# Filling TensorE's pauses with products whose results nobody reads

## The chip, the cores and the metric

The kernel runs on one core of a Trainium2 chip. The metric is the device time of one execution in microseconds. Three timed runs stand for the kernel before: 1015.5, 1013.42 and 1009.02 us, median 1013.42 us.

## The reference, cut to what matters

The kernel computes eight residual layers over x and a context, both 32 x 64 rows of 128 features (2048 tokens): `x = x + layer(layernorm(x), ...)`. In order they are: attention with 16 small heads (A0), a feed-forward layer (F0), attention with 16 heads of 64 (A1), a mixture of 16 experts (E1), two mixtures of eight experts of which every token takes two (E2, E3), attention with 16 small heads under a mask (A3), and a quantised feed-forward layer (Q3). The change sits ahead of E2, in and ahead of E3, and ahead of A3. The two expert layers are, in short:

```
# E2: the routing looks at the context, not at x
logits = context @ Wg + bg                      # 2048 x 8
top 2 of the logits, softmax over the two -> combine
y = relu(x @ W1[e] + b1[e]) @ W2[e] + b2[e];  out = sum_e combine[e] * y[e]
# E3: the routing looks at x
logits = x @ w_router.T;  top 2, weights normalised -> combine
y = (silu(x @ w_gate[e].T) * (x @ w_up[e].T)) @ w_down[e].T
out = sum_e combine[e] * y[e]
# A3: q = x @ Wq.T, k, v = context @ Wk.T, Wv.T; masked softmax attention; @ Wo.T
```

All inputs are float32.

## The kernel before

The 2048 tokens are 16 tiles of 128 tokens (NT), in four groups of four tiles (NG groups of GW = 512 columns). X keeps the residual stream with tokens on the partitions; `ctxT` keeps the context turned, features on the partitions; `ident` is the 128 x 128 identity. Every engine has its own instruction list, written out in full in the order given by hand; engines wait for each other by semaphores only (`wait_ge`), and a waiting instruction holds up everything behind it on its engine. There are eight PSUM banks; `m.banks[4]` is the fifth.

**Layers E2 and E3** are both built by `dispatched_experts`. Each token's two copies are sorted by expert into 39 tiles of 128 rows (NTILE). The normalised rows are stored to DRAM by SyncE's queue, and GpSimd fetches the rows of one tile with an indirect DMA (`fetch`, L2214), three tiles ahead. Per tile TensorE turns the rows (`turn`, L2094), multiplies them by the first weights of the tile's expert (`first`, L2098: four 128-column products in E2, six in E3), and, one tile later, the hidden rows by the last weights (`second`, L2123). VectorE and ScalarE copy the turned rows and the expert's weights, apply the activation and copy the result, and GpSimd sends it to DRAM with an indirect DMA (`send`, L2222). A float32 product shows as two MATMUL records in the trace. At the end SyncE reads the results back, and VectorE adds them to X group by group (L2305), with the next layer's norm statistics between the groups.

For E2 the tables of the routing (which token sits in which row) were made long before, beside F0. For E3 they depend on x, and are made between the layers, in this order on TensorE (the block `if gated:` of `tensor`, from L2075): `m.ahead.keys` (four 512-column products for the keys of A3, banks 2 to 5, copied out by ScalarE at L555), then per group g a turn of the normalised rows (L220, waits for VectorE's `xn`) and four logit products of 8 columns each (L1797, wait for ScalarE's copy of the turned rows, L228); `rank_products` (L1849 to L1851, wait for VectorE's choice of the best two, until L1828); `m.ahead.values` (L569); and `table_products` four times (L1914, eight 40-column products each). Table j waits for GpSimd's `owners` (L1906), which waits for VectorE's `places` (L1894, L1898); `places` of j = 2 and 3 wait for `ab_used` of table j - 2, because two buffers take turns. After the last table ScalarE copies it out (`owner`, L1920), VectorE makes the indices, GpSimd issues the first fetch (671.15 us in the profile), and TensorE waits for those rows in `turn(0)`.

**A3**, `prepared_attention`: TensorE first waits until E3 has written its last output, then takes per group a turn of the normalised rows (L220) and one 512-column product (L632), `queries(g)`, with the scores of tiles 0 and 1 (L642, L648) between them; after that the tiles follow in a steady order.

Of the kernel before, what the change touches and what calls it, by code (L numbers as in the profile page):

```python
# [18 lines left out]
NG = NT // GT  # L19
GW = GT * P  # L20
# [12 lines left out]
def live(t):  # L33

    return not isinstance(t, int) or 0 <= t < NT


def past(t, k):

    return not isinstance(t, int) or t >= k  # L40
# [7 lines left out]
def pipeline(eng, step, lo, hi, end, first=0):  # L48

    for n in range(first, lo):  # L50
        step(n, n % 2)
    with eng.Fori(lo, hi - 1, 2) as i:
        step(i, lo % 2)
        step(i + 1, (lo + 1) % 2)
    for n in range(hi, end):
        step(n, n % 2)
# [18 lines left out]
def apart(eng, m):  # L75


    eng.sem_inc(m.passed, 1)


class Signal:
# [43 lines left out]
class Norm:  # L125
# [10 lines left out]
    def stats(self, dve, x, t, p):  # L136
        if past(t, 2):
            dve.wait_ge(*self.rstd_ready(t - 1))
        dve.bn_stats(self.st[:, p, :], x).then_inc(self.stats_chain.sem, 1)
        dve.wait_ge(*self.stats_chain(2 * t + 1))  # L140
        apart(dve, self)
        dve.bn_aggr(self.mv[:, p, :], self.st[:, p, :]).then_inc(self.stats_chain.sem, 1)
        dve.wait_ge(*self.stats_chain(2 * t + 2))
        dve.tensor_scalar(self.ve[:, p, :], self.mv[:, p, 1:2], EPS, None, ALU.add).then_inc(self.var_ready.sem, 1)  # L144
# [435 lines left out]
def prepared_attention(sh, m, tag, masks, w, ahead):  # L580
# [42 lines left out]
    def tensor(pe):  # L623
        pe.wait_ge(*free)
        pe.wait_ge(*masks)

        def queries(g):
            norm.turn(pe, g)
            pe.wait_ge(*norm.xnT_ready(g + 1))
            if g >= 2:  # L630
                pe.wait_ge(*q_all(g - 1))
            pe.matmul(m.banks[6 + g % 2], w["q"], m.XNT[:, g * GW:(g + 1) * GW], start=True, stop=True  # L632
                      ).then_inc(q_ps.sem, 1)

        def scores(t, p):
            pe.wait_ge(*qT_ready(t + 1))
            pe.wait_ge(*kexp_ready(t + 1))
            if past(t, 2):
                pe.wait_ge(*sub_ready(t - 1))
            apart(pe, m)  # L640
            for u in range(2):
                pe.matmul(pS[p][:, u, :].rearrange("p (h k) -> p h k", k=S), m.hidden_square[:, :],  # L642
                          m.hidden_keys[:, bass.ds(t, 1), :].broadcast_to([P, HP, S]), start=True, stop=False,
                          skip_group_check=True)
            for b in range(2):
                for u in range(2):
                    rows = slice(u * S, (u + 1) * S)
                    mm = pe.matmul(pS[p][b * S:(b + 1) * S, u, :], qT[rows, p, b * S:(b + 1) * S],  # L648
                                   kexp[rows, p, b].rearrange("p h k -> p (h k)"), start=False, stop=True,
                                   skip_group_check=True)  # L650
            mm.then_inc(scores_ready.sem, 1)

        def turn_out(t, p):
            pe.wait_ge(*on_ready(t + 1))
            if past(t, 1):
                pe.wait_ge(*oT_ready(t))
            pe.transpose(J2[:, 0:P], on[:, p, :], m.ident[:, :]).then_inc(oT_ps.sem, 1)

        def weigh_values(t, p):
            pe.wait_ge(*probT_ready(2 * t + 2))  # L660
            pe.wait_ge(*vbd_ready(2 * t + 2))
            if past(t, 1):
                pe.wait_ge(*on_ready(t))
            for c in range(HP):
                for b in range(2):
                    mm = pe.matmul(pO[b * S:(b + 1) * S, c * 18:c * 18 + 18], probT[:, p, c, b * S:(b + 1) * S],
                                   vbd[:, p, b, 2 * c:2 * c + 2, :].rearrange("p h d -> p (h d)"),
                                   start=True, stop=True)
            mm.then_inc(o_ps.sem, 1)

        def project(t, p):
            pe.wait_ge(*oT_ready(t + 1))
            if past(t, 1):
                pe.wait_ge(*x_done(t))
            pe.matmul(J2[:, P:2 * P], oT[:, p, :], w["o"], start=True, stop=True).then_inc(out_ps.sem, 1)

        def turn_probs(t, p):
            pe.wait_ge(*prob_ready(t + 1))
            if past(t, 1):
                pe.wait_ge(*probT_ready(2 * t))  # L680
            for c in range(HP):
                tr = pe.transpose(pP[:, c // 4, c % 4 * P:c % 4 * P + P],
                                  prob[:, p, 2 * c:2 * c + 2, :].rearrange("p h k -> p (h k)"), m.ident[:, :])
                if c % 4 == 3:
                    tr.then_inc(probT_ps.sem, 1)

        def step(n, p):
            q = 1 - p
            if live(n):
                scores(n, p)  # L690
            if live(n - 3):
                turn_out(n - 3, q)
            if live(n - 2):
                weigh_values(n - 2, p)
            if live(n - 3):
                project(n - 3, q)
            if live(n - 1):
                turn_probs(n - 1, q)

        queries(0)  # L700
        queries(1)
        scores(0, 0)
        queries(2)
        scores(1, 1)
        queries(3)
        pe.wait_ge(*q_all(NG))
        turn_probs(0, 0)
        pipeline(pe, step, LO, HI, END, 2)
# [1291 lines left out]
def dispatched_experts(sh, m, tag, start, spec):  # L2000
# [12 lines left out]
    E, C, gated, disp = spec["E"], spec["C"], spec.get("gated"), spec["dispatch"]  # L2013
# [37 lines left out]
    def turned_at(n):  # L2051

        return n - 2 if turns and 0 <= n - 2 < 3 * turns.E else None
# [18 lines left out]
    def tensor(pe):  # L2072
        if spec.get("late"):
            spec["late"].tensor(pe)
        if gated:  # L2075
            m.ahead.keys(pe)
            for g in range(NG):
                norm.turn(pe, g)
                pe.wait_ge(*norm.xnT_ready(g + 1))
                disp.logit_products(pe, J1, m.XNT, spec["wr"], g)  # L2080
            disp.rank_products(pe, J1)
            m.ahead.values(pe)
            for j in range(NCH):
                disp.table_products(pe, J1, j)
            pe.wait_ge(*disp.owner_ready(1))
        m.begin(pe, start)
        pe.wait_ge(*disp.expert_ready(1))
        pe.wait_ge(*spec["weights_here"])

        def turn(i):  # L2090
            pe.wait_ge(*x_here[i % 4](16 * (i // 4 + 1)))
            if i >= 2:
                pe.wait_ge(*xT_ready(i - 1))
            pe.transpose(T[i % 2][:, 0:P], xg[:, i % 4, :], m.ident[:, :]).then_inc(xT_ps.sem, 1)  # L2094

        def products(out, p, k0):
            for c in range(C):
                mm = pe.matmul(out[:, c * P:(c + 1) * P], WE[:, p, (k0 + c) * P:(k0 + c + 1) * P], XT[:, p, :],  # L2098
                               start=True, stop=True)
            mm.then_inc(a_ps.sem, 1)  # L2100

        def first(i):
            p = i % 2
            pe.wait_ge(*xT_ready(i + 1))
            pe.wait_ge(*w_ready(i + 1))
            if gated:
                if i >= 2:
                    pe.wait_ge(*h_ready(i - 1))
                products(m.banks[2 + p], p, 0)
                products(m.banks[4 + p], p, C)  # L2110
            else:
                if i >= 3:
                    pe.wait_ge(*h_ready(i - 2))
                products(m.banks[2 + i % 3], p, 0)

        def second(i):
            p = i % 2
            e = pe.value_load(disp.expert[0:1, i:i + 1], min_val=0, max_val=E - 1)
            pe.wait_ge(*h_ready(i + 1))
            if i >= 2:  # L2120
                pe.wait_ge(*y_out(i - 1))
            for c in range(C):
                mm = pe.matmul(Y[p][:, 0:P], h[:, p, c, :],  # L2123
                               W2[:, bass.ds(e, 1), c, :].rearrange("p o d -> p (o d)"),
                               start=c == 0, stop=c == C - 1)
            mm.then_inc(y_ps.sem, 1)

        turn(0)
        for i in range(NTILE):
            first(i)  # L2130
            if i + 1 < NTILE:
                turn(i + 1)
            if i >= 1:
                second(i - 1)
            if turned_at(i) is not None:
                turns.turn(pe, turned_at(i))
        second(NTILE - 1)
# [895 lines left out]
```

## Time and profile before

| | us |
|---|---|
| median of the three runs (lowest, highest) | 1013.42 (1009.02, 1015.5) |
| the profiled execution | 1012.4 |
| its span, first to last instruction | 1010.6 |
| mean granted TensorE clock | 0.883 of full speed |
| TensorE busy (matmuls) / weight loads | 785.4 / 647.6 |
| VectorE / ScalarE / GpSimd busy | 617.2 / 468.1 / 373.9 |

The span is cut by TensorE's clock into stretches at 1.00 (2.4 GHz) and at 0.50 (1.2 GHz); a mean between the two in a row says that the clock changed in it. In the timeline view each row is one instruction or a run of equal ones: start, duration, engine, source line, what it writes and reads, count, and in brackets the idle time of the engine before it with what ended it. Times are counted from the first instruction of the span. What a product "costs" TensorE is read from the spacing of successive records, since records overlap.

### The profile page before, as it was taken

What the parts mean: (1) busy time and instruction counts of PE and PEld (TensorE: products, weight loads), DVE (VectorE), ACT (ScalarE), POOL (GpSimd) and SP (SyncE); (2) the same over time, 40 slices, a digit from 0 to 9 for tenths busy, and PEclk for the clock granted to TensorE, in tenths of its full rate; (3) what the DMA queues carried; (4) which work ended last, traced back from release to release, by engine and by line L of the source; (5) the groups of instructions that cost most, each with busy time, mean ns of one, the idle gap of its engine ahead of it and who ended that gap; (6) DMA issues with size and microseconds to landing.
All of it is one profiled execution on the core that took longest, in us unless ns stands there. A gap on an engine that the chain in (4) does not pass through costs nothing.

```text
span 1010.6 us, 24103 instructions
## 1 busy us (share of the span) xinstructions
PE 785.4 (78%) x8041; PEld 647.6 (64%) x8041; DVE 617.2 (61%) x1610; ACT 468.1 (46%) x928; POOL 373.9 (37%) x492
## 2 busy tenths in 40 slices
PE   6998898999999789996477765567878469969005
PEld 3776787888888679985476663567777426643005
DVE  3886747777777667767353324642222378867795
ACT  3886434555444344442154433034554237735753
POOL 5663421111111331111566662146666445550800
PEclk9999699999999979999699998569999779978557
DMA  6300000000000000023333213101111300000001
GB/s 186 97 0 1 1 1 3 2 3 1 0 0 3 1 9 21 20 102 103 95 104 87 61 44 102 42 17 40 43 43 44 96 11 3 0 1 1 0 0 42
DMA packets 49218, 36.06 MB, mean 36 GB/s; under 512 B 7665, under 2 KB 44978, under 8 KB 49138
## 3 DMA queue, kind: packets, MB, share of 16 engines
q1 hardware_dynamic: 43420, 24.45, 8.6%
q0 software_dynamic: 4992, 10.23, 3.7%
q8 instruction: 48, 0.79, 0.3%
q10 hardware_dynamic: 726, 0.33, 0.1%
q14 instruction: 32, 0.26, 0.1%
HBM read 26.73 MB, written 8.26 MB: 35 GB/s over the span
## 4 chain that ended last, share of the span: by engine, by line
PE 66%; DVE 12%; issue 6%; another core or an unknown queue 5%; ACT 4%; DMA 3%; DVEq 2%; POOL 2%; ACTq 1%; SPq 0%; POOLq 0%
PE psum L2098 9%; PE psum L1448 7%; PE psum L2123 3%; PE psum L1018 3%; PE psum L960 3%; PE psum L938 3%; PE psum L923 3%; PE psum L2398 2%; PE psum L1415 2%; PE psum L1416 2%; PE psum L1417 2%; PE psum L308 2%; PE psum L1000 2%; PE psum L648 2%
## 5 line engine op out<-in xcount | busy, mean ns | idle before, releaser
L2098 PE MATMUL psum<-E_XT,E_weights 128*128 128x128 f32 x780 | 115.4, 300 | 48.7 <-DVE E_XT L2250 20.0
L2098 PEld LDWEIGHTS psum<-E_XT,E_weights 128*128 128x128 f32 x780 | 103.5, 209 | 58.3 <-DVE E_XT L2250 24.3
L2222 POOL DMA_INDIRECT y_scratch<-E_y,route_place_of x78 | 78.8, 1010 | 78.2 <-DVE E_y L2275 33.1
L2214 POOL DMA_INDIRECT E_rows<-rows_scratch,route_token_of x78 | 76.4, 979 | 31.8 <-issue 25.9
L1707 DVE SCALAR_TENSOR_TENSOR X<-psum,E_gates,X 128x128 f32<-128x128 f32 x256 | 71.7, 344 | 26.3 <-PE psum L1448 26.2
L1448 PEld LDWEIGHTS psum<-E_w,E_h 128*128 128x128 f32 x512 | 69.4, 198 | 11.6 <-issue 3.5
L2178 ACT ACTIVATE E_h<-psum,cols 128x128 f32<-128x128 f32 x156 | 44.6, 368 | 67.0 <-PE psum L2098 45.8
L1532 ACT ACTIVATE E_h<-psum,cols 128x512 f32<-128x512 f32 x64 | 43.9, 689 | 67.4 <-PE psum L1417 67.4
L1448 PE MATMUL psum<-E_w,E_h 128*128 128x128 f32 x512 | 70.3, 282 | 4.8 <-DVE X L1707 3.8
L2265 DVE TENSOR_TENSOR E_h<-E_sg,psum 128x384 f32<-128x384 f32 x39 | 21.6, 554 | 72.7 <-PE psum L2098 27.7
L203 POOL TENSOR_TENSOR rstd<-vareps,nhalf 128x4 f32<-128x4 f32 x24 | 24.7, 1032 | 81.7 <-DVE vareps L197 81.5
L220 PE MATMUL psum<-ident,xn 128*128 128x128 f32 x80 | 19.6, 392 | 39.7 <-DVE xn L211 29.5
L150 POOL TENSOR_TENSOR A_A_inner_rstd<-A_A_inner_vareps,nhalf 128x1 f32<-128x1 f32 x16 | 8.7, 544 | 95.5 <-DVE A_A_inner_vareps L144 95.5
L2123 PE MATMUL psum<-L1w,E_h 128*128 x312 | 43.5, 284 | 0.5 <-DVE E_y L2277 0.5
L220 PEld LDWEIGHTS psum<-ident,xn 128*128 128x128 f32 x80 | 13.3, 202 | 47.0 <-issue 23.2
L2387 PE MATMUL psum<-ident,Q_amax_rows 128*1 128x128 f32 x5 | 1.8, 352 | 52.3 <-DVE Q_amax_rows L2495 51.6
L773 POOL TENSOR_TENSOR A_kexp<-E_first,hmask 128x512 f32<-128x512 f32 x32 | 32.6, 1042 | 25.8 <-PE psum L648 25.7
L2123 PEld LDWEIGHTS psum<-L1w,E_h 128*128 128x128 f32 x312 | 39.5, 198 | 1.1 <-issue 0.7
L2094 PE MATMUL psum<-ident,E_rows 128*128 128x128 f32 x78 | 22.9, 294 | 22.2 <-DMA E_rows<-rows_scratch,route_token_of 22.2
L2161 ACT ACTIVATE E_weights<-E_first 128x768 f32 x39 | 32.9, 843 | 14.0 <-issue 13.7
L2277 DVE TENSOR_TENSOR E_y<-psum,E2b2all 128x128 f32<-128x128 f32 x39 | 11.3, 290 | 44.7 <-PE psum L2123 19.8
L1563 POOL CAST E_WH<-E_w 128x128 fp32r<-128x128 f32 x16 | 4.6, 290 | 90.9 <-DMA E_w<-in_L_ffn_routed_w 72.3
(342 smaller groups left out, 2156.1 us busy)
## 6 DMA issues: line engine op xcount, KB each, us to landing
routed_back<-y_scratch SPq DMA_DIRECT2D x16, 256.0 KB, 4.9
E_first<-in_L_xattn_W SPq DMA_DIRECT2D x1, 2048.0 KB, 8.5
L1w<-in_L_xattn_W SPq DMA_DIRECT2D x8, 256.0 KB, 4.5
rows_scratch<-xn SPq DMA_DIRECT2D x8, 256.0 KB, 2.3
E_w<-in_L_ffn_routed_w SPq DMA_DIRECT2D x28, 64.0 KB, 1.8
E_raw<-in_L_ffn_w_down SPq DMA_DIRECT2D x8, 176.0 KB
E_rows<-rows_scratch,route_token_of POOLq DMA_INDIRECT x78
y_scratch<-E_y,route_place_of POOLq DMA_INDIRECT x78
```

The lines of the kernel that those rows point to most:

```text
L220: tr = pe.transpose(self.bank[:, i * P:(i + 1) * P], self.m.xn[:, g * GT + i, :], self.m.ident[:, :])
L773: ke = pool.tensor_tensor(kexp[:, p, b], kk.broadcast_to([P, HP, S]), m.hmask[:, :].rearrange("p (h o) -> p h o", o=1).broadcast_to([P, HP ...
L923: mm = pe.matmul((J1, J0)[j][:, c * P:(c + 1) * P], w["k"][:, cc * P:(cc + 1) * P], columns(m.ctxT, t, P), start=True, stop=True)
L1448: mm = pe.matmul(y_bank(e, g)[:, i * P:(i + 1) * P], h[:, g % 2, c, i * P:(i + 1) * P], w2[:, p, c, :], start=(c == 0 and i == 0), stop=(c ...
L1532: act.activation(h[:, g % 2, c, :], ring[(C * g + c) % 4], spec["func"], bias=spec["b1"][:, bass.ds(e * C + c, 1)]).then_inc(h_ready.sem, 1)
L1707: st = dve.scalar_tensor_tensor(out=m.X[:, t, :], in0=y_bank(e, g)[:, i * P:(i + 1) * P], scalar=gates[:, t, bass.ds(e, 1)], in1=m.X[:, t, :],
L2098: mm = pe.matmul(out[:, c * P:(c + 1) * P], WE[:, p, (k0 + c) * P:(k0 + c + 1) * P], XT[:, p, :], start=True, stop=True)
L2123: mm = pe.matmul(Y[p][:, 0:P], h[:, p, c, :], W2[:, bass.ds(e, 1), c, :].rearrange("p o d -> p (o d)"), start=c == 0, stop=c == C - 1)
L2161: act.activation(WE[:, i % 2, :], W1[:, bass.ds(e, 1), :].rearrange("p o f -> p (o f)"), ACT.Copy).then_inc(w_ready.sem, 1)
L2178: ac = act.activation(h[:, p, c, :], m.banks[2 + i % 3][:, c * P:(c + 1) * P], spec["func"], bias=spec["b1"][:, bass.ds(e * C + c, 1)])
L2214: pool.indirect_dma_start(out=xg[:, i % 4, :], out_offset=None, in_=rows[:, :], in_offset=bass.IndirectOffsetOnAxis(ap=disp.token_of[:, i: ...
L2222: pool.indirect_dma_start(out=yrows[:, :], in_=y[:, i % 3, :], in_offset=None, out_offset=bass.IndirectOffsetOnAxis(ap=disp.place_of[:, i: ...
```

## The change

A helper issues n products `ident x ctxT[:, 0:512]` into bank 4, float32, each a start and a stop, with no semaphore. Nobody reads the result. It is called at nine places of TensorE's list. One wait is added, for ScalarE's copy of the four key blocks, ahead of the first products of E3's block, since bank 4 holds one of those blocks.

```diff
--- before.py
+++ after.py
@@ -76,6 +76,12 @@
 
 
     eng.sem_inc(m.passed, 1)
+
+
+def idle_products(pe, m, n):
+
+    for _ in range(n):
+        pe.matmul(m.banks[4], m.ident[:, :], m.ctxT[:, 0:GW], start=True, stop=True)
 
 
 class Signal:
@@ -697,7 +703,9 @@
             if live(n - 1):
                 turn_probs(n - 1, q)
 
+        idle_products(pe, m, 12)
         queries(0)
+        idle_products(pe, m, 2)
         queries(1)
         scores(0, 0)
         queries(2)
@@ -2074,13 +2082,19 @@
             spec["late"].tensor(pe)
         if gated:
             m.ahead.keys(pe)
+            pe.wait_ge(*m.ahead.k_ready(NG))
+            idle_products(pe, m, 8)
             for g in range(NG):
+                idle_products(pe, m, (0, 2, 2, 0)[g])
                 norm.turn(pe, g)
                 pe.wait_ge(*norm.xnT_ready(g + 1))
                 disp.logit_products(pe, J1, m.XNT, spec["wr"], g)
+            idle_products(pe, m, 5)
             disp.rank_products(pe, J1)
             m.ahead.values(pe)
             for j in range(NCH):
+                if j:
+                    idle_products(pe, m, 2)
                 disp.table_products(pe, J1, j)
             pe.wait_ge(*disp.owner_ready(1))
         m.begin(pe, start)
@@ -2125,6 +2139,7 @@
                                start=c == 0, stop=c == C - 1)
             mm.then_inc(y_ps.sem, 1)
 
+        idle_products(pe, m, 6 if gated else 12)
         turn(0)
         for i in range(NTILE):
             first(i)
```

In the last hunk E3 (gated) gets 6 products and E2 gets 12.

## Rows read from the trace of the kernel before

**Rows 1.** The page: granted TensorE clock in 40 slices, and chain shares by engine.

```profile
PEclk9999699999999979999699998569999779978557
...
PE 66%; DVE 12%; issue 6%; another core or an unknown queue 5%; ACT 4%; DMA 3%; DVEq 2%; POOL 2%; ACTq 1%; SPq 0%; POOLq 0%
```

**Rows 2.** Busy time by stretch (us, instructions), PEclk the mean clock; half-clock stretches.

```profile
475.50:499.40 23.90, 6.62 (x28) 5.96 (x29) 11.68 (x43) 2.29 (x8) 9.99 (x9) 0.50 0.38 106
...
799.80:823.70 23.90, 7.94 (x18) 3.40 (x22) 18.18 (x83) 2.39 (x4) 10.39 (x15) 0.50 0.33 91
sum 95.60, PE 40.94 PEld 33.04 DVE 57.76 ACT 13.74 POOL 31.23; mean PE 10.23 PEld 8.26 DVE 14.44 ACT 3.44 POOL 7.81
```

**Rows 3.** The same view, of pauses of TensorE that began at full clock.

```profile
366.90:370.00 3.10, 0.09 (x1) 0.12 (x1) 2.85 (x12) 1.92 (x3) 0.74 (x2) 0.95 0.15 42
...
742.10:745.30 3.20, 0.48 (x3) 0.49 (x4) 0.56 (x1) 0.94 (x3) 2.00 (x3) 0.98 0.13 41
...
583.40:586.10 2.70, 0.26 (x2) 0.27 (x3) 0.97 (x3) 0.53 (x3) 1.87 (x2) 1.00 0.16 49
```

**Rows 4.** Timeline (start us, us, engine, line, instruction, [idle before]), start of layer E2.

```profile
478.73 1.11 DVE L1707 SCALAR_TENSOR_TENSOR X<-psum,E_gates,X 128x128 f32<-128x128 f32 x4
...
492.02 0.45 PE L2094 MATMUL psum<-ident,E_rows 128*128 128x128 f32 x1 [18.04 <-DMA E_rows<-rows_scratch,route_token_of]
...
492.84 2.08 PE L2098 MATMUL psum<-E_XT,E_weights 128*128 128x128 f32 x8 [0.38 <-DVE E_XT L2250]
...
497.60 1.92 PE L2123 MATMUL psum<-L1w,E_h 128*128 x8
...
500.24 1.01 POOL L2222 DMA_INDIRECT y_scratch<-E_y,route_place_of  x1 [3.89 <-DVE E_y L2277]
```

**Rows 5.** Timeline: four 512-column products at full clock.

```profile
618.93 3.70 PE L549 MATMUL psum<-ctxT,L3w 128*128 128x512 f32 x8 [0.58 <-ACT qw_down L2661]
```

**Rows 6.** Busy time by stretch, of 512-column products that began at half clock.

```profile
910.40:915.80 5.40, 5.31 (x7) 2.21 (x8) 2.80 (x8) 1.19 (x2) 0.00 (x0) 0.50 0.00 0
```

**Rows 7.** Timeline of the routing ahead of layer E3 and of its first tile.

```profile
622.67 0.60 ACT L555 ACTIVATE E_first<-psum 128x512 f32<-128x512 f32 x1 [0.26 <-PE psum L549]
...
632.12 1.12 PE L220 MATMUL psum<-ident,xn 128*128 128x128 f32 x4 [9.48 <-DVE xn L211]
...
641.64 1.11 PE L220 MATMUL psum<-ident,xn 128*128 128x128 f32 x4 [1.09 <-DVE xn L211]
...
646.95 1.87 PE L1797 MATMUL psum<-cols,XNT 128*128 128x8 f32 x8 [0.69 <-ACT XNT L228]
...
653.97 0.80 PE L1849 MATMUL psum<-route_both,earlier 128*128 128x128 f32 x2 [5.15 <-DVE route_ahead L1828]
...
655.35 5.96 PE L569 MATMUL psum<-L3w,ctxT 128*64 128x64 f32 x128
...
661.75 1.07 PE L1914 MATMUL psum<-route_A,route_B 128*128 128x40 f32 x8 [0.44 <-POOL route_A L1906]
...
666.28 3.39 PE L1914 MATMUL psum<-route_A,route_B 128*128 128x40 f32 x16 [2.13 <-POOL route_A L1906]
...
673.87 0.45 PE L2094 MATMUL psum<-ident,E_rows 128*128 128x128 f32 x1 [4.21 <-DMA E_rows<-rows_scratch,route_token_of]
...
674.69 2.93 PE L2098 MATMUL psum<-E_XT,E_weights 128*128 128x128 f32 x12 [0.37 <-ACT E_XT L2155]
...
681.41 1.50 PE L2098 MATMUL psum<-E_XT,E_weights 128*128 128x128 f32 x12
```

**Rows 8.** Timeline, start of the last attention.

```profile
813.56 1.09 PE L220 MATMUL psum<-ident,xn 128*128 128x128 f32 x4 [15.95 <-DVE xn L211]
...
820.03 2.07 PE L632 MATMUL psum<-XNT,L3w 128*128 128x512 f32 x2 [0.69 <-ACT XNT L228]
...
824.26 0.66 PE L220 MATMUL psum<-ident,xn 128*128 128x128 f32 x4
...
825.61 1.12 PE L632 MATMUL psum<-XNT,L3w 128*128 128x512 f32 x2 [0.69 <-ACT XNT L228]
```

## The prediction

> **What bounds the kernel now.** I began with the page. In the chain that ended last, TensorE holds 66% of the span, and its granted clock is at full speed in most slices but low in some [rows 1]. So a lower clock can cost time only where TensorE's own work lies on that chain, and the next view asks how much of it there is. The view by stretch, over the four half-clock stretches next to the changed places (475.5 to 499.4, 625.7 to 659.8, 666.6 to 680.3, 799.8 to 823.7 us), shows 95.6 us, of which TensorE works 40.9 us [rows 2]. In the rest it waits: for row fetches, for VectorE's norms, for VectorE's and GpSimd's routing chain. If all 40.9 us were at full clock and all of it on the chain, 20.4 us would be saved. That is the ceiling, and the added products have to be paid out of it.
>
> Next, what comes before a fall. TensorE's last product before E2 ended at 474.0 (492.02 less 18.04 of idle, [rows 4]) and the clock was at half from 475.5 [rows 2]. Pauses of 3.1 us (366.8) and 2.8 us (742.0) end with the mean clock just under 1.00: it had fallen by their end. A pause of 2.5 us (583.3) passed at 1.00 [rows 3]. I read it so: a pause of 3 us or more mostly costs the clock, one of 2 to 2.5 us sometimes. And a rise: 512-column products begun at half clock ran 5.4 us without one [rows 6], and E2's first tiles from 492.0 ran until 499.4, 7.4 us [rows 2, 4]. I take 5 us of dense products before a rise, between 2.5 (no row excludes half of rows 6) and 7.4.
>
> **Price of one product.** Four of the same shape took 3.70 us at full clock [rows 5]: 0.86 us each without the tail of the last. At half clock seven records started in 5.4 us, two records a product [rows 6]: 1.72 us each. Twelve take 10.3 us at full, 20.6 at half. If they start at half and the clock rises after t us, they take 10.3 + t/2. Nobody reads them, but TensorE works in order: whatever does not fit the pause delays the real work behind it, and half clock doubles the overhang.
>
> **E2, 12 products.** TensorE is let go when the last update of X ends, 479.9 [rows 4], at half clock, and its rows arrive at 492.02: 12.1 us. With t = 5 the products end at 492.7, 0.7 us late (t = 2.5: 0.4 early, so on time; t = 7.4: 1.9 late; no rise: 8.5 late). At full clock the first tiles gain: twelve records take 1.50 instead of 2.93 us [rows 7], so eight gain 0.95, and two firsts (2.08 each) and one second (1.92) lie in a row to the first output [rows 4]: 2.8 us. GpSimd's first send waited 3.89 us for that output, and its later fetches stand behind that send [rows 4], so the gain is kept. Net -2.0, ends -2.8 and +7.
>
> **Keys, 8 products and the added wait.** The keys are copied out at 623.3 [rows 7]. Still at full clock, eight products end at 630.2; the first turn waits for VectorE until 632.12 [rows 7]. Cost nothing, covered by that pause. The wait holds only the products; the pause hides it.
>
> **Logits, 0/2/2/0.** On the path are the last two groups, from the turn at 641.64 to the last logit at 648.8 [rows 7]. At full clock the turn takes 0.66 instead of 1.11 [rows 7, 8]; the 8-column logits, 1.87 at half, come near the table products, eight narrow records in 1.07 [rows 7]: I take 1.0. Twice both: -2.6. But from 630.2 to 634.4 TensorE has only a turn and narrow products, so the clock may fall; then the two products ahead of group 2 take 3.4 us where the pause was 1.09 [rows 7], 2.3 late. Between -2.6 and +2.3 I take -1.0, nearer to full clock because products of group 1 follow.
>
> **Rank, 5 products.** The pause is 5.15 us [rows 7]; 4.3 fit at full, 8.6 at half are 3.4 late, and full clock saves 0.6 of the small products. Between -0.6 and +3.4: +0.3.
>
> **Tables, 2 products ahead of each but the first.** This is the step that decides. The values (128 records, 5.96 us mostly at half) become about 3 us at full, but the first table still waits for VectorE and GpSimd, 7.8 us behind the rank products (653.97 to 661.75, [rows 7]). A new pause of about 3 us opens, of the kind after which the clock had fallen [rows 3]. Then the pairs stand in the way: before, table 1 followed table 0 at once, and all four took from 661.75 to 669.67, 7.9 us, the last two at half [rows 7]. Tables now, at full throughout: 4 x 1.07 + 3 x 1.72 = 9.4, +1.5. At half throughout: 4 x 1.70 + 3 x 3.44 = 17.1, +9.2 (16 records in 3.39, [rows 7]). With a rise after 5 us, behind the first pair: 1.7 + 3.44 + 3 x 1.07 + 2 x 1.72 = 11.8, +3.9. I take +3.9; the ends are +1.5 and +9.2. Behind them wait ScalarE's copy, VectorE's indices and GpSimd's first fetch. Even at full clock this step loses.
>
> **E3, 6 products.** The pause is 4.21 us [rows 7]; 5.2 at full is 1.0 late, 10.3 at half 6.1 late: +1.1. The first tile's product falls from 2.93 to 1.50 [rows 7], partly hidden behind ScalarE's activation: -1.0 (ends 0 and -2.8, with the second tile).
>
> **A3, 12 and 2 products.** TensorE is free at 797.6 (813.56 less 15.95, [rows 8]). At full clock twelve end by 808.3. The turn waits until 813.56, a pause of 5.2 us, longer than those after which the clock had fallen: it starts at half as before. Turn, query product and the pair fill from there, so the rise comes near 819 instead of 823.7 [rows 2]; the pair (begun near 817.0) makes the second turn, at 818.2 before, some 1.5 us late. From there to the third turn, 824.26, half-clock work on the path shrinks by about 2.2 us (0.45 for a turn, 0.95 for a product, 2.07 against 1.12, the rest scores) [rows 8]. Net -0.7, ends -2.0 (clock held) and +2.2 (no rise sooner).
>
> **Sum.** -2.0 - 1.0 + 0.3 + 3.9 + 1.1 - 1.0 - 0.7 = +0.6 us, on the profiled execution's 1012.4 (span 1010.6 and 1.8 around it): 1013.0. That execution lies 1.0 below the median of the three runs, which is what is predicted: 1014.0.
>
> **A rule against the rows.** Rows first: of the 95.6 us at half, TensorE works 40.9 [rows 2]. The Trainium skill, page "TensorE: Matmul & The Clock Gate", section "Terms", says the penalty is about the throttled time times (1 - K/N). By that rule, an estimate, these four stretches cost 47.8 us and the time without them would be near 966 us.
>
> **Rivals.**
> *The clock is held.* If narrow products and short pauses do not let it fall, every stage ends at its low end: -2.8 (E2), -2.6 and -0.6 (routing), +1.5 (tables), +1.0 - 1.4 (E3), -2.0 (A3): -6.9, 1006.5. For it: pauses of 2.5 us passed [rows 3]. Against it: the pauses of 3 us before the tables and 5.2 us in A3 stay. 20%.
> *Slower: the half clock meets the products of the routing.* Place: from the logits of group 2 to the last table. If the clock falls between 630.2 and 641.6 and is back only in the tables: +2.3, +3.4, +3.9, +1.1 - 1.0, with -2.0 and -0.7 elsewhere: +7.0, 1020.4. It decides as soon as the pair ahead of group 2 runs at half. If the tables stay at half as well, 5.3 more and six products at half, 5.1 more: 1031. For it: the trace has half clock in all of this stretch. Against it: the products themselves are dense. 18%, of which 5% for the longer form.
> *All half-clock work was on the chain.* Then 20.4 us go: 993.6. Against it stand the waits of rows 4 and 7. The same rule of the skill points this way, only further. 3%.
> *It doesn't do what it says.* If these products do not raise the clock, E2 is 8.5 late, and the tables and the six products cost 9.2 and 6.1: about +25, 1039. Against it: the same shape stands before the rise of rows 6. 2%.
>
> **How the numbers follow.** My forecast has 57% with its own range of 1010 to 1018.5 (steps' ends, and runs that spread from 1009.0 to 1015.5). The range of 8 in 10 reaches to both rivals: 1007.0 to 1020.0. One per cent, about what a measurement of this kernel can tell from no change, is 10 us: all low ends together give 6.9, so faster 4% (the third rival and a rest); slower 8% (the long form of the second, the fourth and a rest); within 88%.
>
> **What would show it.** In the changed trace: first turn of E2 within 1 us of 492.7 and eight-record products near 1.1 us at once; eight products done 2 us before the first turn of E3's routing; the clock row between rank and tables, at half when the first table starts; more than 9.4 us from the first table's start to the last one's end; the six products overhanging the row fetch; half clock at A3's first turn and a rise before 821. Wrong would be: full clock from 623 to 680 without a break, or a first tile of E2 still at 2.08 us.

## The result and the profile after

The changed kernel took 1021.25 us in the median of 19 runs, the kernel before 1015.61 us in 19 runs on the same chip: ratio 1.0043, 95% interval 1.0029 to 1.0058, or 4.4 us slower (2.9 to 5.9). A second copy of it (below) gave 1.0025 (1.0004 to 1.0046). Ratios and intervals are those of the record, taken over all runs; the quotient of the two medians is 1.0056. The forecast was 0.6 us slower, 1014.0 in a range of 1007.0 to 1020.0; 1013.42 us times the ratio is 1017.8. One run each of two variants below (e2_sixteen, fitted), 1205 us long at a mean clock of 0.63 and 0.64, is left out of their ratios as slow.

First the page of the changed kernel: the granted clock in 40 slices, the chain that ended last by engine, and by line.

```profile
PEclk9999699999999879998999989798899889978557
...
PE 72%; DVE 10%; ACT 4%; issue 4%; another core or an unknown queue 3%; POOL 2%; DMA 2%; DVEq 2%; ACTq 1%; SPq 0%; POOLq 0%
PE psum L2112 10%; PE psum L1456 7%; PE psum L2137 5%; PE psum L84 4%; PE psum L1026 3%; PE psum L968 3%; PE psum L946 3%; PE psum L931 3%; PE psum L2413 2%; PE psum L1423 2%; PE psum L1424 2%; PE psum L1425 2%; PE psum L314 2%; PE psum L1008 2%
...
L84 PE MATMUL psum<-ctxT,ident 128*128 128x512 f32 x110 | 60.0, 700 | 7.3 <-DVE X L1715 5.9
```

The clock is higher than before, 0.906 against 0.883 on average, and TensorE's share of the chain went from 66% [rows 1] to 72%. L84 is the line of the added products: 55 of them, two records each, 60.0 us of TensorE, and 4% of the chain, some 40 us, is the products themselves. Products that nobody reads became part of what sets the time.

Where the half clock was next to the changed places (95.6 us, TensorE at work in 40.9 [rows 2]), the same view of the changed kernel shows this (busy time and records of PE, PEld, DVE, ACT, POOL, then the mean clock):

```profile
478.00:488.20 10.20, 5.97 (x7) 2.52 (x8) 9.43 (x38) 0.00 (x0) 4.03 (x3) 0.50 0.26 77
641.80:645.20 3.40, 3.40 (x7) 1.39 (x6) 3.15 (x16) 0.00 (x0) 1.03 (x1) 0.50 0.11 30
648.60:655.50 6.90, 6.90 (x15) 3.80 (x16) 4.68 (x16) 0.00 (x0) 0.00 (x0) 0.51 0.01 2
665.70:669.10 3.40, 3.40 (x10) 1.86 (x8) 1.24 (x2) 0.00 (x0) 0.72 (x1) 0.50 0.00 0
822.70:829.50 6.80, 6.11 (x12) 2.57 (x11) 6.59 (x29) 1.19 (x2) 2.53 (x3) 0.50 0.00 0
sum 30.70, PE 25.78 PEld 12.14 DVE 25.08 ACT 1.19 POOL 8.31; mean PE 5.16 PEld 2.43 DVE 5.02 ACT 0.24 POOL 1.66
```

65 us of half clock went here, and the kernel became slower. (Over the whole span it is some 45 us less, 237 against 192; the bodies of E2 and E3 have more of it than before, 10.2 and 27.3 us against 3.5 and 17.1.) In the half clock that is left TensorE works 84% of the time, against 43% before. But 20.7 of its 25.8 us are the added products, by the same view of L84 alone:

```profile
sum 30.70, PE 20.67 PEld 7.44; mean PE 4.13 PEld 1.49
```

So the kernel's own work at half clock fell from 40.9 to 5.1 us, and what now runs at half clock is mostly the products themselves, some of them in the way of the chain. The rule of the Trainium skill weighed in the prediction (page "TensorE: Matmul & The Clock Gate", section "Terms") would have it that 64.9 us less throttled time are worth about 32 us, an estimate by that page; no run shows a gain of this size or any gain of the whole change.

The start of E2, TensorE's timeline:

```profile
482.23 13.52 PE L84 MATMUL psum<-ctxT,ident 128*128 128x512 f32 x24 [5.93 <-DVE X L1715]
495.59 0.27 PE L2108 MATMUL psum<-ident,E_rows 128*128 128x128 f32 x1
496.25 1.16 PE L2112 MATMUL psum<-E_XT,E_weights 128*128 128x128 f32 x8 [0.38 <-issue]
...
499.01 1.15 PE L2137 MATMUL psum<-L1w,E_h 128*128 x8
500.05 1.16 PE L2112 MATMUL psum<-E_XT,E_weights 128*128 128x128 f32 x8
```

Against [rows 4], the eight-record products take 1.16 instead of 2.08 us at once. But the turn now has no idle time before it: the twelve products end 13.4 us after E1 does (482.2), where the rows had arrived after 12.2. Then the routing:

```profile
625.96 7.13 PE L84 MATMUL psum<-ctxT,ident 128*128 128x512 f32 x16 [0.69 <-ACT E_first L561]
634.42 0.66 PE L226 MATMUL psum<-ident,xn 128*128 128x128 f32 x4 [1.33 <-DVE xn L217]
...
636.68 1.96 PE L84 MATMUL psum<-ctxT,ident 128*128 128x512 f32 x4
639.19 0.66 PE L226 MATMUL psum<-ident,xn 128*128 128x128 f32 x4 [0.55 <-DVE xn L217]
...
641.45 3.41 PE L84 MATMUL psum<-ctxT,ident 128*128 128x512 f32 x4
644.66 0.88 PE L226 MATMUL psum<-ident,xn 128*128 128x128 f32 x4
...
650.05 7.22 PE L84 MATMUL psum<-ctxT,ident 128*128 128x512 f32 x10
657.11 0.38 PE L1857 MATMUL psum<-route_both,earlier 128*128 128x128 f32 x2
...
657.77 3.95 PE L575 MATMUL psum<-L3w,ctxT 128*64 128x64 f32 x128
664.18 1.07 PE L1922 MATMUL psum<-route_A,route_B 128*128 128x40 f32 x8 [2.46 <-POOL route_A L1914]
665.10 3.17 PE L84 MATMUL psum<-ctxT,ident 128*128 128x512 f32 x4
667.28 2.26 PE L1922 MATMUL psum<-route_A,route_B 128*128 128x40 f32 x8
669.38 1.96 PE L84 MATMUL psum<-ctxT,ident 128*128 128x512 f32 x4
...
673.39 1.37 PE L1922 MATMUL psum<-route_A,route_B 128*128 128x40 f32 x8
675.05 5.42 PE L84 MATMUL psum<-ctxT,ident 128*128 128x512 f32 x12 [0.29 <-ACT route_owner L1928]
680.31 0.27 PE L2108 MATMUL psum<-ident,E_rows 128*128 128x128 f32 x1
680.95 1.60 PE L2112 MATMUL psum<-E_XT,E_weights 128*128 128x128 f32 x12 [0.37 <-ACT E_XT L2170]
```

Only two of these groups of products, the eight and the pair of group 1, leave a pause behind them. The five (7.22 us from start to end, at half clock in large part) run past 655.3, when VectorE had the ranks' operand ready; the values fell from 5.96 [rows 7] to 3.95 us, and the 2.46 us pause that this opens is followed by a fall of the clock at 665.7, in the first pair; the tables last from 664.18 to 674.8, 10.6 us against 7.9 [rows 7].

### The profile page after: what moved, and what is told of

The parts are those of the page before. It is cut to its first block, busy times and chain, and to the rows that moved or that the text cites. A ratio compares the mean times of both kernels' runs of the same rounds, so it can differ in the third digit from the quotient of the medians.

```text
span 1019.7 us, 24322 instructions
## 1 busy us (share of the span) xinstructions
PE 834.9 (82%) x8151; PEld 666.3 (65%) x8151; DVE 617.4 (61%) x1610; ACT 466.8 (46%) x928; POOL 372.5 (37%) x492
## 4 chain that ended last, share of the span: by engine, by line
PE 72%; DVE 10%; ACT 4%; issue 4%; another core or an unknown queue 3%; POOL 2%; DMA 2%; DVEq 2%; ACTq 1%; SPq 0%; POOLq 0%
PE psum L2112 10%; PE psum L1456 7%; PE psum L2137 5%; PE psum L84 4%; PE psum L1026 3%; PE psum L968 3%; PE psum L946 3%; PE psum L931 3%; PE psum L2413 2%; PE psum L1423 2%; PE psum L1424 2%; PE psum L1425 2%; PE psum L314 2%; PE psum L1008 2%
## 5 line engine op out<-in xcount | busy, mean ns | idle before, releaser
L84 PE MATMUL psum<-ctxT,ident 128*128 128x512 f32 x110 | 60.0, 700 | 7.3 <-DVE X L1715 5.9
L84 PEld LDWEIGHTS psum<-ctxT,ident 128*128 128x128 f32 x110 | 23.3, 220 | 35.5 <-issue 26.9
L2292 DVE TENSOR_TENSOR E_y<-psum,E2b2all 128x128 f32<-128x128 f32 x39 | 11.3, 290 | 53.8 <-PE psum L2137 43.2
L156 POOL TENSOR_TENSOR A_A_inner_rstd<-A_A_inner_vareps,nhalf 128x1 f32<-128x1 f32 x16 | 8.7, 543 | 95.6 <-DVE A_A_inner_vareps L150 95.6
L781 POOL TENSOR_TENSOR A_kexp<-E_first,hmask 128x512 f32<-128x512 f32 x32 | 32.6, 1042 | 25.9 <-PE psum L654 25.8
L1067 ACT ACTIVATE A_xnT<-psum,cols 128x128 f32<-128x128 f32 x16 | 7.3, 457 | 65.3 <-PE psum L956 65.3
```

The lines of the kernel that those rows point to most:

```text
L84: pe.matmul(m.banks[4], m.ident[:, :], m.ctxT[:, 0:GW], start=True, stop=True)
L781: ke = pool.tensor_tensor(kexp[:, p, b], kk.broadcast_to([P, HP, S]), m.hmask[:, :].rearrange("p (h o) -> p h o", o=1).broadcast_to([P, HP ...
```

## Experiments

**How they are read.** Every variant was measured beside the kernel before, in five rounds. Besides the ratio, each profile gives the lengths of stages: **start of E2** (end of E1 to the third tile's first product), **body** of E2 and E3 (from there to the last second product), **routing** (end of the keys to E3's third tile), **start of A3** (E3's last second product to the first turned probabilities). The 14 profiles (before, after and twelve variants; two of the twelve are second copies) show how far one profile can be trusted. The part ahead of E2, the same in all, ends between 477.9 and 482.7 us. E2's body is 116.3 to 121.3 us long, E3's 114.4 to 120.3, in kernels with and without products. So the 9.1 us between the spans of the first two profiles (1010.6 and 1019.7) hold 2.3 us from before anything was changed. Part of the scatter of E2's body goes with the clock inside it: the two shortest (116.3 and 117.0 us) have 3.4 and 3.5 us of half clock in them, the two longest (121.2 and 121.3) have 17.1, and over the 14 profiles the correlation is 0.86; for E3's body it is 0.44. Short stretches scatter less and decide below.

**1 to 3. Each place alone.** Theory R put the loss into the routing ahead of E3. Rival B put it into the bodies: what a start gains, the layer's later tiles give back.

```
e2_only:      idle_products(pe, m, 0 if gated else 12)   # nothing else
routing_only: 8 behind keys, (0,2,2,0), 5, 2 if j, 6 ahead of E3
a3_only:      12 ahead of queries(0), 2 ahead of queries(1)
```

> Only the 12 products ahead of layer E2's first turn. Theory R (the loss is made in the routing ahead of E3, the other places gain): from the end of E1 to the start of the third tile's first product 1.5 to 2 us less than in the kernel before (there 19.5 us), E2's body after that as before (117.0 us from that start to the last second product), total -1.5 to -2 us, ratio 0.998. Rival B (an earlier start is given back in the body of a sparse layer, because each of its tiles then meets the clock or a queue at a worse moment): the start gains the same, the body is 1 to 2 us longer, total within 0.5 us of before, ratio 1.000.

> Only the products and the wait between E2 and E3 (8, 2, 2, 5, 2, 2, 2, 6). Theory R: from the end of the keys to the end of the tables 47.0 us becomes 49 to 51, to E3's first turn 51.2 becomes 54 to 56, E3's third tile 2 to 4 us later than before, the body of E3 as before (116.2 us from the third tile's first product to the last second product), total +3 to +4 us, ratio 1.003 to 1.004. Rival B: besides, E3's body is 3 to 4 us longer, total +6 to +8 us, ratio 1.007.

> Only the 12 and 2 products ahead of the last attention's queries. Both theories: the clock falls in the pause that the twelve leave (4.7 us in the changed kernel's trace), the pair delays the second turn by about 2 us, and the earlier rise gives it back: from E3's last product to the first turn of probabilities 33.7 us before, 33.0 to 33.6 now; total -0.7 to 0 us, ratio 0.9995. If the clock is held the same stretch takes 32 us, ratio 0.998.

Measured: e2_only 1.0009 (0.9989 to 1.0029), routing_only 1.0010 (0.9991 to 1.0029), a3_only 1.0007 (0.9986 to 1.0027). No ratio differs from 1, and their sum, +2.6 us, is compatible with the whole. Two forecasts were missed: e2_only did not gain its 1.5 to 2 us (0.998), and the routing alone, forecast at 1.003 to 1.004, has an interval that ends at 1.0029. So these three ratios do not place the loss. The stages say more. e2_only: start 17.8 us against 19.5 before, body 121.2 against 117.0. That looked like rival B, but a3_only, where E2 is untouched, had a body of 120.0. routing_only: routing 60.9 against 58.8.

**4. Without the pairs between the tables.**

```
-                if j:
-                    idle_products(pe, m, 2)
```

> The changed kernel without the pairs of products between the four tables; all else stays. Theory R: the four tables, 10.6 us in the changed kernel's trace (7.9 before), take 6 to 8 us again, E3's first turn comes 3 us earlier than in the changed kernel, total 3 us below it, ratio to before 1.001. Rival B: E3's body stays 3 to 4 us longer than before, total 2 to 4 us above before, ratio 1.003.

Measured: 1.0007 (0.9992 to 1.0023) against 1.0043 with them. The three pairs cost 3.6 us, the difference of these ratios, 2.1 either way by their two intervals; against the second copy (1.0025) it is 1.8, 2.7 either way, so the time alone does not fix the size. The tables' own length does it better: 10.6, 10.6 and 13.9 us in the three profiles with the pairs, 7.9 to 8.1 in the ten without products there. From table 0 to the end of the tables it is 8.0 us again here. Something is given back, though: from the end of the tables to E3's third tile 13.1 us against 11.6 with the pairs.

**5. The kernel before again.** One comment added.

> The kernel before once more, only a comment added. Nothing can differ, so it says what the profiled body of a sparse layer (from the third tile's first product to the last second product) is from one execution to the next. Theory N (the bodies fall into patterns of their own that differ by chance): ratio within 0.2% of 1; E2's body between 116.9 and 121.3 us, and not the 116.98 us of the first profile except by luck. Rival B (an earlier start of E2 is given back in its body, by a wait that the start had covered): E2's body within 0.5 us of 116.98 us, since the start is not moved.

Measured: 0.9997 (0.9977 to 1.0017). E2's body: 119.3 us, 2.3 more than in the first profile of the same code. Rival B's evidence, one body against another, is gone; most of that difference goes with the half clock in the body (3.5 us in the first profile, 13.7 here, 17.1 in e2_only). The start of E2, too, moved without products: 18.4 us instead of 19.5. The clock rose 17.1 us after E1's end and not 19.6: in the second of three half-clock products.

**6. Twelve products ahead of E2, again.**

> Only the twelve products ahead of E2, once more. Theory N: the first product of the third tile again 1.3 us nearer to the end of E1 than before (about 17.8 us), the body anywhere between 117 and 121.3 us, the time on average 1.3 us shorter: ratio 0.9987, and with the first run of it an interval that still holds that. Rival B: the body again 121 us or more, the ratio at or above 1.000.

Measured: 0.9988 (0.9968 to 1.0009); with e2_only a mean of 0.9999, about 0.0014 either way, which neither shows nor excludes a gain of 1.3 us. Start 17.8, body 118.3.

**7. Fours between the tables, nothing else.**

```
+                if j:
+                    idle_products(pe, m, 4)
```

> Only the products between the tables, and four instead of two ahead of the second, third and fourth table; nothing elsewhere. Theory R (the pairs between the tables are the loss): twelve products in the way of the tables instead of six. 12 x 0.86 = 10.3 us at full clock, less the 3.7 us or so that faster tables give back, so 6 to 9 us slower: ratio 1.006 to 1.009, and keys' end to tables' end 53 to 56 us against 47.0 before. Rival (E2's and E3's bodies decide, the pairs hardly count): less than 3 us slower, ratio under 1.003.

Measured: 1.0061 (1.0040 to 1.0082), 6.2 us slower; end of the keys to end of the tables 54.9 us against 47.0. Both numbers are as Theory R had them, but of the 7.9 us 1.7 arose ahead of any added product: VectorE waited 7.88 us for the rows read back, not 6.16, and TensorE's first turn came later, as this kernel's rows show. The first is to be held against the 9.48 us of [rows 7]:

```profile
634.66 1.12 PE L226 MATMUL psum<-ident,xn 128*128 128x128 f32 x4 [11.21 <-DVE xn L217]
664.29 1.07 PE L1920 MATMUL psum<-route_A,route_B 128*128 128x40 f32 x8 [1.50 <-POOL route_A L1912]
676.98 1.36 PE L1920 MATMUL psum<-route_A,route_B 128*128 128x40 f32 x8
```

The tables themselves took 14.1 us, 5.9 more than the 8.1 of most profiles without products there, and this agrees with the 6.2 us of time. Products between the tables go into the time.

**8. Fitted to the pauses of the changed profile.**

```
A3: 12 and 2 -> 17 and 0;  E3: 6 -> 4;  routing: none;  E2: 12
```

> A version fitted to the pauses that the profile after shows: twelve products ahead of E2, none in the routing, four ahead of E3, seventeen ahead of the first query turn of the last attention (the pause from 807.0 to 822.3 us holds 17 x 0.86 = 14.6 us) and none ahead of the second. Theory R: E2 -1.3, E3's four products at the fetch wait 0 to +0.5 with a first tile 1 us faster, A3 -1.5 to -2: 1 to 4 us faster than before, ratio 0.996 to 0.999. Rival B (what a start gains the body gives back): ratio 1.000 +/- 0.001.

Measured: 1.0002 (0.9977 to 1.0026); the gain forecast did not come. In the last attention the seventeen did what they were to do, TensorE's timeline:

```profile
798.07 14.86 PE L84 MATMUL psum<-ctxT,ident 128*128 128x512 f32 x34 [0.38 <-DVE E_y L2283]
813.35 0.66 PE L226 MATMUL psum<-ident,xn 128*128 128x128 f32 x4 [0.43 <-DVE xn L217]
814.70 1.13 PE L638 MATMUL psum<-XNT,L3w 128*128 128x512 f32 x2 [0.69 <-ACT XNT L234]
818.12 1.11 PE L226 MATMUL psum<-ident,xn 128*128 128x128 f32 x4 [2.30 <-DVE xn L217]
...
824.66 0.66 PE L226 MATMUL psum<-ident,xn 128*128 128x128 f32 x4
```

The first query product takes 1.13 us, not 2.07, and all it buys is a longer wait for VectorE: 2.30 us ahead of the second turn. The third turn comes 27.0 us after E3's last product; before, 26.7. VectorE's timeline of the kernel before says why:

```profile
821.86 2.36 DVE L211 TENSOR_SCALAR xn<-X,meanvar,rstd 128x128 f32<-128x128 f32 x8
824.48 1.22 DVE L837 TENSOR_REDUCE A_mx<-psum 128x16 f32<-128x1024 f32 x1 [0.25 <-PE psum L648]
```

VectorE is busy with the norms until 824.2 and takes up the scores 0.25 us later. Up to that point all of TensorE's half-clock work had at most 0.25 us to give.

**9. Sixteen ahead of E2.** The question is whether a shift of the start reaches the end.

```
idle_products(pe, m, 0 if gated else 16)   # nothing else
```

> Only products ahead of E2, sixteen instead of twelve, so that the first turn comes 4 x 0.86 = 3.4 us later than with twelve. With twelve the third tile's first product began 17.8 us after the end of E1 in every profile, in those without products 18.4 to 19.5; with sixteen it should be at 21.2. Rival B (the start of E2 is not what paces its body, so a shift of the start is taken back within some tiles): the fourteenth tile's first product at 53.7 to 55 us after the end of E1, as in all profiles so far with and without products (53.7 to 54.6), and the time within 2 us of before, ratio 0.999 to 1.002. Theory K (a shift of the start is kept): the fourteenth tile at 57 us or more, 3.4 us slower than with twelve, ratio about 1.003.

Measured: 1.0033 (1.0013 to 1.0053), 3.3 us slower; the third tile at 21.2, the fourteenth at 56.9 against 52.8 to 54.6 in all others. Rival B falls: a delay of E2's start is kept. What of a gain? With twelve or ten products the third tile comes at 17.6 to 17.9 us in all seven profiles (mean 17.8), without them at 18.4 to 19.5 (six profiles, mean 19.1): 1.3 us. At the fourteenth tile the means are 53.8 and 54.3, so 0.6 us of the 1.3 is still there.

**10. The six products ahead of E3, alone.**

```
idle_products(pe, m, 6 if gated else 0)    # nothing else
```

> Only the six products ahead of E3. Forecast term: they end 1 us after the rows would have let the first turn start and the first tiles gain 1.0, net +0.1. Theory R: from the end of the tables to the third tile's first product 11 to 12 us, as in the profiles without them (10.7 to 11.7), ratio 1.000 +/- 0.001. Rival (the six products run at half clock, in which case they take 10.3 us against a pause of 4.2): that stretch 13 us or more, as in the profile without the table pairs (13.1), ratio 1.001 to 1.002, and E3's body a matter of chance (114.4 to 120.3 us so far) in both.

Measured: 1.0032 (1.0010 to 1.0054), 3.2 us slower: the rival by its stretch (14.0 us from the end of the tables to the third tile), and above the 1.001 to 1.002 that it gave for the time. Stretches with the six products in this kernel, and then in the changed one (the mean clock stands behind the five busy times):

```profile
669.90:677.70 7.80, 7.73 (x13) 3.28 (x13) 1.08 (x6) 0.86 (x2) 3.91 (x4) 0.68 0.16 36
```

```profile
675.00:680.40 5.40, 5.35 (x13) 2.34 (x13) 1.07 (x6) 0.84 (x1) 3.24 (x4) 1.00 0.09 24
```

The same six products take 5.4 us at full clock and 7.8 from half. From GpSimd's first fetch to the first turn: 2.7 us without them, 4.1 in the changed kernel, 6.5 here; the first tiles give back 1.0 in both. With the pairs between the tables, which cost 3.6, the six ran at full clock; without them part of the six ran at half (5.6 us from the first fetch in experiment 4). This is what was given back there.

**11. What seemed worth having.**

```
E2: 10;  keys: 8;  logits: (0,2,2,0);  rank, tables, E3, A3: none
```

> What the profiles so far leave as worth having: ten products ahead of E2 (with twelve the first turn started as the last of them ended, 1.2 us after the rows would have let it), eight behind the keys and 0/2/2/0 ahead of the groups of logits, and none ahead of rank, tables, E3 and the last attention. Theory R: from the end of the keys to the end of the logits 24.9 to 25.1 us as with those products before (25.7 to 26.2 without), and with nothing ahead of rank the gain reaches the end of the tables: 45.8 us against 46.7 to 47.3. Third tile of E2 at 16.2 to 17 us after E1's end. If all of it is kept, 1.1 + 2.2 us faster, ratio 0.997; if E2's share is given back in the body (Rival B), 1.1 us, ratio 0.999.

Measured: 0.9978 (0.9956 to 1.0000), 2.2 us faster at the edge of what five rounds tell, and the only variant whose whole interval lies at or below 1. Its profile shows two things. With ten products the first turn comes 12.1 us after E1's end and not 13.4, yet the third tile is at 17.6, as with twelve. VectorE's copy of the third tile's rows, in this kernel and then in e2_again:

```profile
497.63 0.29 DVE L2260 COPY E_XT<-psum 128x128 f32<-128x128 f32 x1 [1.95 <-remote]
```

```profile
497.69 0.29 DVE L2257 COPY E_XT<-psum 128x128 f32<-128x128 f32 x1 [0.66 <-PE psum L2100]
```

Both start 17.3 to 17.4 us after E1's end (480.36 and 480.28), against 17.7 to 18.0 in the profiles without products there. ScalarE's next activation starts with them, at 497.71 and 497.76, though its products had ended at 496.0 and 497.1. In all seven profiles with twelve or ten products it is 17.3 to 17.5, wherever the first turn was. Two engines are held there together, and the profile does not name the source. The expectation of 16.2 to 17 us for the third tile was missed by this. And the logits, TensorE's timeline:

```profile
623.02 7.13 PE L84 MATMUL psum<-ctxT,ident 128*128 128x512 f32 x16 [0.69 <-ACT E_first L561]
...
632.90 1.76 PE L1803 MATMUL psum<-cols,XNT 128*128 128x8 f32 x8 [0.69 <-ACT XNT L234]
634.51 3.76 PE L84 MATMUL psum<-ctxT,ident 128*128 128x512 f32 x4
638.06 1.06 PE L226 MATMUL psum<-ident,xn 128*128 128x128 f32 x4
639.81 1.87 PE L1803 MATMUL psum<-cols,XNT 128*128 128x8 f32 x8 [0.69 <-ACT XNT L234]
641.54 3.76 PE L84 MATMUL psum<-ctxT,ident 128*128 128x512 f32 x4
```

Here both pairs ran at half clock (3.76 us, not 1.96), and the logits ended 27.8 us after the keys, where 24.9 to 25.1 was expected and 25.9 is usual without products: the same products that gained 0.8 to 1.8 us in four other profiles lost 1.9 in this one. (This is the profiled execution, 1013.3 us; the median of this variant's runs is 1010.3.)

**12. The changed kernel again.**

> The changed kernel once more, only a comment added. Theory R: ratio 1.003 to 1.006 again; from the end of the keys to E3's third tile 61 us (58.3 on average without the products); E3's start to the last attention's first turned probabilities 33.5 to 34.2 us as in every profile. The bodies of E2 (116.99 to 121.28 so far) and E3 (114.35 to 120.29) anywhere in their spread; Rival (the products lengthen E3's body, 120.29 in the first profile of it): E3's body at 118 or more again.

Measured: 1.0025 (1.0004 to 1.0046). Routing 62.6 us; E3's body 116.3, so the rival on that body is not borne out; start of A3 33.5. The tables of this execution:

```profile
657.58 1.52 PE L1922 MATMUL psum<-route_A,route_B 128*128 128x40 f32 x8 [2.46 <-POOL route_A L1914]
658.93 3.76 PE L84 MATMUL psum<-ctxT,ident 128*128 128x512 f32 x4
661.70 2.52 PE L1922 MATMUL psum<-route_A,route_B 128*128 128x40 f32 x8
664.05 3.76 PE L84 MATMUL psum<-ctxT,ident 128*128 128x512 f32 x4
...
670.14 1.36 PE L1922 MATMUL psum<-route_A,route_B 128*128 128x40 f32 x8
```

Two pairs at half clock, 13.9 us for the tables, where the first profile had one and 10.6.

## Why the prediction was right, and where its sizes were off

The mechanism held: less half clock, no time gained, and the loss in the routing, most of it between the tables. This rests on experiments 4, 7 and 10 and on the lengths of stages; the routing alone (1.0010) does not show it in time. The time was missed by 4 us (2 by the second copy). Taken term by term, with the mean of the profiles that have a set of products and of those that lack it:

| term | forecast | measured |
|---|---|---|
| E2, 12 products | -2.0 | -1.3 at the third tile, -0.6 at the fourteenth; in time, over both runs, -0.2, 1.4 either way |
| keys, 8 products and the wait | 0 | 0: done 1.3 us before the first turn |
| logits | -1.0 | -1.3 in four profiles, +1.9 in one, against those without products (table_fours, with its late rows, left out) |
| rank, 5 products | +0.3 | +1.3 |
| values at full clock, to table 0 | 0 | -0.7 |
| pairs between the tables | +3.9 | +3.6 (three profiles; in time 3.6 against the first copy, 1.8 against the second) |
| six products, first tiles of E3 | +1.1 - 1.0 | +1.35 - 1.0; alone 3.7 - 1.0 |
| A3 | -0.7 | -0.1 (5 against 9 profiles) |

**The routing** was right as a sum: -1.0 + 0.3 + 3.9 + 0.1 is +3.3, and end of the keys to E3's third tile is 58.2 us in the six profiles without products there and 61.5 in the three with all of them, +3.35. Pairs ahead of the tables cost what was said, by the mechanism said: a pause opens behind the faster values, the clock falls, the pairs stand in front of work that used to follow at once. The price goes with the count (3.6 us for six products, 5.9 for twelve, experiment 7). The term for the rank was mis-sized: the trace had part of the five at half clock, and their last product ended 0.7 to 1.8 us past the operand, of which 0.7 came back because the first table then follows the rank products after 7.1 and not 7.8 us.

**E2's start** was mis-sized and is the first part of what is missing. I let the products overhang by 0.7; it was 1.2 in three of the profiles with twelve and 0.1 in the others. It goes with the clock's rise, which came 5.9 to 6.0 us after E1's end in those three and 3.7 to 3.8 us after it in the others; I had taken 5. And I took the gain of three half-clock records in a row, 2.8 us, as all on the chain. It is cut off at the third tile, whose rows VectorE copies at 17.3 to 17.5 us whatever TensorE did before. Also, before is not always as bad as its first profile: that start was 18.4 to 19.5 in unchanged code. "The gain is kept" was half wrong; "a delay is kept" is shown (experiment 9).

**A3** was mis-sized from a row that was there to read: TensorE's half-clock records lay beside VectorE's norms, which run until 824.2. The gain had a ceiling of 0.25 us and I took 0.7, with 2.0 as an end.

By these terms the sum is -0.6 (E2) + 3.35 - 0.1, about +2.7; the runs say +4.4 (2.9 to 5.9) and +2.5 (0.4 to 4.6). The second agrees, the first leaves 1.7 us. Whether these 1.7 us of the first comparison are E3's body (mean 117.6 us in the six profiles with products just ahead of it, 116.4 in eight without, in a scatter of 1.4 to 1.8; the longest, 120.3 in the first profile of the change, also has the most half clock in it, 27.3 us) or chance stays open. The three largest errors of the sum (E2, the rank, A3) all point the same way, towards too small a loss; the range was wide enough to hold them.

**Readings.** One reading of the trace was off: at the pause of 742.0 [rows 3] the clock had not fallen by the pause's end, 744.8, but fell 0.4 us behind it. The E2 products at t = 2.5 are 0.6 early, not 0.4, and the third rival starts from 1014.0 where the first two start from 1013.4. None of this changes a term of the sum.

**Rivals.** "The clock is held" (1006.5) did not happen. "The half clock meets the products of the routing" (1020.4) did in part: its place was right, and pairs at half clock are in each profile of the changed kernel, one of them ahead of group 2, the point from which it was to decide. Which products meet the half clock changes from one execution to the next, so forecast and rival are not two cases but two ends of one scatter. "All half-clock work on the chain" is refuted: the kernel's own work at half clock in these stretches fell from 40.9 to 5.1 us, at no gain.

**What would show it.** First turn of E2 at 495.6, 13.4 after E1's end, where 12.8 was forecast (492.7): within 1 us. Eight products done before the first turn: by 1.3 us, not 2. "Half clock when the first table starts": no, it fell 1.5 us after that start (665.7) in the first profile, and within the first table in the second (1.52 us instead of 1.07). Over 9.4 us for the tables: yes, 10.6. The six over the row fetch: yes. A3's first turn at half clock was 0.76 us, nearly full; the clock fell at 822.7 in it, and the rise came at 829.5, 7.2 us after that turn began, where 5.5 was forecast (819 less 813.6).

## What to carry to other kernels

Half clock in a pause costs nothing, and half clock beside another engine's longer work costs nothing; before paying for warm-up, find the first row behind the slow work that waits for TensorE alone, and take its idle time (here 0.25 us in A3) as the ceiling. Filler products belong where the pause behind them is longer than they are at half clock, never between two steps of a chain: there six products, 5.2 us long at full clock, cost 3.6 us, and twelve, 10.3 us long, cost 6.2. And a stage of some 117 us that differs by up to 4 us between two executions of the same kernel, and by 5 to 6 over the 14 profiles, cannot be judged from one profile; fix on short stretches and on the ratio.

## What the runs showed of the hardware

**The same product costs by when it meets the clock.** The pair ahead of the logits of group 1 took 1.96 us in the changed kernel and 3.76 in the fitted one, the pair ahead of group 2 3.41, 2.99 (second copy) and 3.76. Five kernels have the same products from the keys to the logits, and in them the clock first fell 10.7, 11.9, 16.1, 16.5 and 17.1 us after the end of the keys. The fall comes at no fixed place of the program, so 1 to 2 us of a pair's price differ from one execution to the next.

**The clock fell soon behind dense products.** In the changed kernel eight products (7.1 us) and a pair 3.6 us behind them did not keep it through the logits: it was at half from 641.8. In the fitted kernel the eight had ended at full clock at 630.15, and it fell at 633.0, with a turn of the rows and the first of the eight-column logits in between; the pair behind them ran at half throughout. In between lay pauses of TensorE (1.4 and 0.7 us) as well as narrow products, and no run separates the two.

**A faster TensorE opens a pause, and the clock falls earlier.** Values at full clock took 3.95 us instead of 5.96, the pause behind them grew from 0.44 to 2.46 us, and the clock fell at 665.7, 1.5 us after the pause had ended. In the four profiles with that pause of 2.46 us the fall came 37.5 to 40.4 us after the end of the keys; in the nine with 0.4 to 1.6 us and no products behind it, 41.0 to 44.9.
